# The level product of a fused convolution and attention kernel: fp32 products against three passes of rounded parts

## The reference

```python
x_aux = silu(conv1x1(gn(x), w_sta))                    # 128 channels
y1 = [x_aux]; y2 = [x_aux]
for _ in range(3):
    y1.append(0.9 * maxpool5(y1[-1]) + 0.1 * sumpool5(y1[-1]) / 25)
    y2.append(exp_weighted_pool5(y2[-1]))              # sum(e*x) / (sum(e) + 1e-6)
y = concat(silu(conv1x1(concat(y1), w_cv1)), silu(conv1x1(concat(y2), w_cv2)))
a = conv1x1(ddwv(ddwh(dwv(dwh(y)))), w_c1)             # four depthwise 3-tap convolutions first
x = x + silu(conv1x1(y * a, w_cvend))
f = tokens(gn(x))                                      # 1024 tokens of 256 channels
x = x + softmax((f @ w1.T) @ f.T / 16) @ (f @ w2.T)
```

## Time and profile before

| | us |
|---|---|
| median of 3 runs | 1432.04 |
| lowest, highest | 1429.85, 1433.74 |
| the profiled execution, its time | 1429.68 |
| the profiled execution, its span | 1427.9 |
| TensorE busy | 1273.4 (89%) |
| VectorE busy | 1148.8 (80%) |
| ScalarE busy | 704.6 (49%) |
| GpSimd busy | 159.5 (11%) |

### The profile page before, as it was taken

How to read it: one execution, slowest core, us unless ns; L and a number is a source line. 1 busy time by engine, 2 the same in 40 slices (tenths; PEclk the granted TensorE clock), 3 DMA queues, 4 the chain that set the end, 5 groups by cost and what they waited for, 6 DMA issues and landing times.

```text
span 1427.9 us, 18374 instructions
## 1 busy us (share of the span) xinstructions
PE 1273.4 (89%) x7162; PEld 1063.4 (74%) x7162; DVE 1148.8 (80%) x1217; ACT 704.6 (49%) x762; POOL 159.5 (11%) x76
## 2 busy tenths in 40 slices
PE   3569899836999998999899989999999999999697
PEld 1249899524878877987798679868986898688597
DVE  7879888595899879877987799779987988786443
ACT  0256768550365347435653566346534653564243
POOL 1657677100000000000000000000000000000000
PEclk9879999867999999999999999999999999999899
DMA  7311212110000100020002000200020002000000
GB/s 291 147 45 75 89 75 106 42 59 0 30 15 1 75 29 15 0 73 29 15 0 103 0 15 15 88 15 0 15 88 15 0 15 88 0 1 36 25 1 30
DMA packets 19176, 62.84 MB, mean 44 GB/s; under 512 B 1601, under 2 KB 4289, under 8 KB 19137
## 3 DMA queue, kind: packets, MB, share of 16 engines
q1 hardware_dynamic: 18432, 62.00, 11.5%
q10 hardware_dynamic: 704, 0.30, 0.1%
HBM read 36.61 MB, written 25.17 MB: 43 GB/s over the span
## 4 chain that ended last, share of the span: by engine, by line
PE 59%; issue 14%; DVE 14%; ACT 6%; DMA 0%; DVEq 0%; ACTq 0%; POOLq 0%; POOL 0%
PE slot L1126 21%; PE slot L1164 12%; PE ps_o L1164 9%; DVE between L1439 5%; PE slot L549 3%; PE slot L1180 3%; DVE a L1439 2%; PE slot L1104 2%; PE ps_e L549 2%; PE ps_ey L565 2%; PE slot L1151 1%; PE ps_ey L549 1%; DVE ps_e L766 1%; DVE x_all L773 1%; PE ps_t L642 1%
## 5 line engine op out<-in xcount | busy, mean ns | idle before, releaser
L1164 PE MATMUL slot<-f_all,q_all 128*128 128x512 f32 x768 | 195.4, 406 | 13.4 <-ACT pooled L1305 13.4
L1164 PE MATMUL ps_o<-v_all,pt_all 128*128 128x256 f32 x1536 | 199.1, 286 | 5.4 <-ACT mixed L1324 5.2
L1164 PEld LDWEIGHTS ps_o<-v_all,pt_all 128*128 128x128 f32 x1536 | 188.7, 191 | 7.7 <-DVE pt_all L1443 6.2
L1164 PEld LDWEIGHTS slot<-f_all,q_all 128*128 128x128 f32 x768 | 144.1, 193 | 43.6 <-ACT pooled L1305 14.8
L1439 DVE SCALAR_TENSOR_TENSOR a<-between,k_columns,a 128x992 f32<-128x992 f32 (+1 forms) x128 | 157.4, 1231 | 4.9 <-ACT a L1296 2.6
L1056 POOL TENSOR_TENSOR c_rstd<-c_spread,k_minus_half 128x2 f32<-128x2 f32 x8 | 5.6, 697 | 1087.0 <-DVE gmean L1509 1087.0
L1319 ACT CAST v_all<-y 128x1024 fp32r<-128x1024 f32 x32 | 33.7, 1052 | 184.6 <-DVE y L1470 184.6
L1443 DVE TENSOR_TENSOR pt_all<-slot,pt_all 128x1024 fp32r<-128x1024 f32 x64 | 78.1, 1221 | 46.9 <-ACT pt_all L1310 46.9
L1104 PE MATMUL slot<-wide,k_cv 128*128 128x512 f32 x256 | 114.3, 597 | 0.0
L1324 ACT ACTIVATE mixed<-ps_o,row_inv 128x256 f32<-128x256 f32 x64 | 30.3, 473 | 150.1 <-PE ps_o L1164 150.1
L1296 ACT ACTIVATE a<-between,k_columns 128x1024 f32<-128x1024 f32 x64 | 79.4, 1241 | 48.6 <-DVE between L1439 47.7
(11 more groups left out here) (166 smaller groups left out, 2725.0 us busy)
## 6 DMA issues: line engine op xcount, KB each, us to landing
levels<-x_all SPq DMA_DIRECT2D x32, 512.0 KB, 2.6
x_all<-in_x SPq DMA_DIRECT2D x8, 1024.0 KB, 13.3
q_all<-levels SPq DMA_DIRECT2D x8, 1024.0 KB, 4.9
x<-in_x SPq DMA_DIRECT2D x8, 1024.0 KB, 4.9
out<-x SPq DMA_DIRECT2D x8, 1024.0 KB, 3.9
pooled<-levels SPq DMA_DIRECT2D x8, 512.0 KB, 3.3
wide<-levels SPq DMA_DIRECT2D x7, 512.0 KB, 3.2
x_all<-in_w_c SPq DMA_DIRECT2D x2, 512.0 KB, 3.6
```

Source lines behind the costliest of these rows:

```text
L1164: last = nc.tensor.matmul(out, lhs, rhs, start=(n == 0), stop=(n == len(parts) - 1))
```

## The change

The `cv1` weights are split like the others into `cv1_hi` and `cv1_lo`: their load goes into a free half of image 5 behind the store of image 3, the scalings run on that copy after the last SiLU, then the cast, and GpSimd makes the low part last. Their fp32 copy is gone. In the third stage `cv1` becomes a `product_split` of 24 passes per tile, with `means()` behind the seventh of its twelve pairs. Level 0 is the pooled part 0, which is split already. Levels 1 to 3 are split at the end of the step before, three casts on ScalarE and three subtractions on VectorE, into v_all and pt_all (free once `cvend` is through); for image 0 this happens ahead of the steps. For level 0 to last through `cv1`, the buffers of two pairs are swapped: the pooled parts 0 and 2 now lie in q_all, 1 and 3 in f_all. The first low part of the taps in a step waits for the end of `cv1`. The scratch for dynamic DMAs is halved.

```diff
--- before.py
+++ after.py
@@ -48,8 +48,8 @@
 COLUMNS = {"b_sta": 1, "b_cv1": CT, "b_cv2": CT, "b_cvend": CT, "b_c1": KT,
            "taps": STAGES * KT * 3, "b_taps": STAGES * KT}
 
-SPLIT = {"w1": (CT, C), "w2": (CT, C), "cvend": (KT, C), "c1": (KT, C4), "cv2": (KT, C)}
-STAGED = {"w1": (0, 1, 0, 512), "w2": (0, 1, 512, 1024), "cvend": (1, 2, 0, 1024), "c1": (2, 4, 0, 1024), "cv2": (4, 5, 0, 1024)}
+SPLIT = {"w1": (CT, C), "w2": (CT, C), "cvend": (KT, C), "c1": (KT, C4), "cv2": (KT, C), "cv1": (KT, C)}
+STAGED = {"w1": (0, 1, 0, 512), "w2": (0, 1, 512, 1024), "cvend": (1, 2, 0, 1024), "c1": (2, 4, 0, 1024), "cv2": (4, 5, 0, 1024), "cv1": (5, 6, 0, 1024)}
 EXP_LN, SILU = "natural_log_exp_and_others", "silu_and_others"
 
 
@@ -116,6 +116,8 @@
         self.hi_done = counted("hi", LEVELS)
         self.lo_done = counted("lo", LEVELS)
         self.boxed = counted("boxed", LEVELS)
+        self.level_hi_done = counted("level_hi", LEVELS)
+        self.level_lo_done = counted("level_lo", LEVELS)
         self.borders = ctx.enter_context(nc.semaphore("chain_borders"))
         self.gate = ctx.enter_context(nc.semaphore("chain_gate"))
         self.n_borders = 2 + 2
@@ -231,6 +233,18 @@
                                                     image2d(self.work_b[:, :]), ALU.mult, ALU.add))
         own.wait()
 
+    def split_into(self, hi, lo):
+        self.hi, self.lo = hi, lo
+
+    def level_split_hi(self, act, i, level):
+        wait(act, self.done, i, MIX * level)
+        self.nc.scalar.copy(self.hi[:, level], self.wide[:, level]).then_inc(self.level_hi_done.sem, 1)
+
+    def level_split_lo(self, dve, i, level):
+        wait(dve, self.level_hi_done, i, level)
+        self.nc.vector.tensor_tensor(self.lo[:, level], self.wide[:, level], self.hi[:, level].bitcast(F32),
+                                     ALU.subtract).then_inc(self.level_lo_done.sem, 1)
+
     def mixture_of_sums(self, dve, level):
         wait(dve, self.summed, 0, 6 * (level + 1))
         self.mixture(dve, 0, level, self.sum_b[:, :, :])
@@ -250,7 +264,7 @@
     def __init__(self, ctx, nc, levels, chain):
         self.nc, self.chain = nc, chain
         self.second = ctx.enter_context(nc.sbuf_tensor("pooled", [P, N], F32))
-        self.shared = ctx.enter_context(nc.sbuf_tensor("q_all", [P, KT, N], F32R))
+        self.shared = ctx.enter_context(nc.sbuf_tensor("f_all", [P, KT, N], F32R))
         self.other = None
         self.second_in = Signal(ctx.enter_context(nc.semaphore("pooled_second_in")), 16)
         self.others_in = Signal(ctx.enter_context(nc.semaphore("pooled_others_in")), 16)
@@ -321,7 +335,7 @@
         ps_var = ctx.enter_context(nc.psum_tensor("ps_var", [P, HALF], F32))
 
         x_in = [sem(f"a_x_in{i}") for i in range(B)]
-        sta_in, cv1_in, box_in = sem("a_sta_in"), sem("a_cv1_in"), sem("a_box_in")
+        sta_in, box_in = sem("a_sta_in"), sem("a_box_in")
         weights_in = {k: sem(f"a_{k}_in") for k in SPLIT}
         stats_done = sem("a_stats_done")
         mv_done = sem("a_mv_done")
@@ -355,19 +369,24 @@
             for i in range(B):
                 sp.dma_start(x_all[:, i], x_v[i]).then_inc(x_in[i], 16)
             sp.dma_start(box_raw[:, :], consts["box"]).then_inc(box_in, 16)
-            sp.dma_start(keep["cv1"][:, :, :], rows("cv1")).then_inc(cv1_in, 16)
-            for k in SPLIT:
+            def load_weights(k):
                 sp.wait_ge(xn_done, STAGED[k][1] * CT)
                 n = STAGED[k][1] - STAGED[k][0]
                 for j in range(n):
                     sp.dma_start(raw[k][:, j].rearrange("p (t o) -> p t o", o=SPLIT[k][1]),
                                  w[k].rearrange("(n t p) o -> n p t o", p=P, n=n)[j]).then_inc(weights_in[k], 16)
 
+            for k in SPLIT:
+                if k != "cv1":
+                    load_weights(k)
+
             for n in range(B):
                 sp.wait_ge(stem_done, n + 3)
                 if n == 0:
                     sp.dma_start(chain.wide[:, 0], x_all[:, 0, 0]).then_inc(chain.loaded.sem, 16)
                 sp.dma_start(levels[n], x_all[:, n, 0]).then_inc(stored[n], 16)
+                if n == 3:
+                    load_weights("cv1")
 
         @block.scalar
         def _(act):
@@ -392,9 +411,6 @@
             act.wait_ge(chain.borders, chain.n_borders)
             chain.zero_first(act)
             silu(3)
-            act.wait_ge(cv1_in, 16)
-            for k in range(1, KT):
-                nc.scalar.mul(keep["cv1"][:, k], keep["cv1"][:, k], T_POOL ** k).then_inc(scaled_done, 1)
             split("w1")
             split("w2")
             silu(4)
@@ -404,6 +420,12 @@
             silu(6)
             split("cv2")
             silu(7)
+            act.wait_ge(weights_in["cv1"], 16)
+            for k in range(1, KT):
+                part = raw["cv1"][:, 0, k * C:(k + 1) * C]
+                nc.scalar.mul(part, part, T_POOL ** k).then_inc(scaled_done, 1)
+            act.wait_ge(scaled_done, KT - 1)
+            split("cv1")
             act.wait_ge(box_in, 16)
             nc.scalar.copy(box[:, :], box_raw[:, :]).then_inc(box_ready, 1)
             chain.zero_next(act, 1)
@@ -460,7 +482,7 @@
             inverse_deviations(1)
             chain.box_sums(pool, 0, 0)
             low_parts(("w1", "w2"))
-            low_parts(("cvend", "c1", "cv2"))
+            low_parts(("cvend", "c1", "cv2", "cv1"))
 
         @block.vector
         def _(dve):
@@ -821,7 +843,7 @@
 
 def kept_tensors(ctx, nc):
 
-    shapes = {"ident": [P, P], "group": [P, P], "cv1": [P, KT, C],
+    shapes = {"ident": [P, P], "group": [P, P],
               "columns": [P, sum(COLUMNS.values())], "minus_half": [P, B * CT]}
     keep = {k: ctx.enter_context(nc.sbuf_tensor("k_" + k, v, F32)) for k, v in shapes.items()}
     at = 0
@@ -885,9 +907,9 @@
 
 
 
-        f_all = sb("f_all", [P, KT, N], F32R)
-        q_all = pooled.shared
-        pooled.other = f_all
+        f_all = pooled.shared
+        q_all = sb("q_all", [P, KT, N], F32R)
+        pooled.other = q_all
         v_all = sb("v_all", [P, KT, N], F32R)
         pt_all = sb("pt_all", [P, KT, N], F32R)
         f_hi, f_lo = f_all[:, 0:CT], f_all[:, CT:KT]
@@ -895,6 +917,7 @@
         v_hi, v_lo = (v_all[:, k:k + CT].rearrange("p t (m c) -> p (t m) c", c=C) for k in (0, CT))
         pt_hi, pt_lo = pt_all[:, 0:2], pt_all[:, 2:4]
         a_hi, a_lo, y_hi, y_lo = f_all, q_all, v_all, pt_all
+        chain.split_into(v_all, pt_all)
         prob = pooled.second
         mixed = sb("mixed", [P, 2, C])
         between = sb("between", [P, 2, N])
@@ -1093,27 +1116,14 @@
                     box_sum(nc, pe, box, slot, zt_hi, zt_lo,
                             (chain.lo_done.sem, chain.lo_done.at(i, level + 1))).then_inc(chain.boxed.sem, 1)
 
-                def cv1(m, between=None):
-
-                    slot = claim("cv", CT + m)
-                    for h in range(2):
-                        for k in range(KT):
-                            if m == 0 and h == 0 and k:
-                                wait(pe, chain.done, i, MIX * k)
-                            rows = chain.wide[:, k, h * HALF:(h + 1) * HALF]
-                            last = nc.tensor.matmul(slot[:, h * HALF:(h + 1) * HALF], keep["cv1"][:, k, cols(m)], rows,
-                                                    start=(k == 0), stop=(k == KT - 1))
-                        if h == 0 and between:
-                            between()
-                    last.then_inc(cv.sem, 1)
-
                 def cols(m):
                     return slice(m * P, (m + 1) * P)
 
-                def product_split(kind, m, name, hi, lo, sig, order, hi_ready, lo_ready):
+                def product_split(kind, m, name, hi, lo, sig, order, hi_ready, lo_ready, between=None):
 
 
                     slot = claim(kind, m)
+                    m = m % CT if kind == "cv" else m
                     w_hi, w_lo = keep[name + "_hi"][:, :, cols(m)], keep[name + "_lo"][:, :, cols(m)]
                     parts = ((w_hi, hi, hi_ready), (w_lo, hi, hi_ready), (w_hi, lo, lo_ready))
                     uses = [(n, part) for part in parts for n in range(KT - 1)] + [(KT - 1, part) for part in parts]
@@ -1125,6 +1135,8 @@
                             hs = slice(h * HALF, (h + 1) * HALF)
                             last = nc.tensor.matmul(slot[:, hs], weights[:, k], inputs(k)[:, hs],
                                                     start=(at == 0), stop=(at == len(uses) - 1))
+                        if between and at == len(uses) // 2:
+                            between()
                     last.then_inc(sig.sem, 1)
 
                 def tiles_of(t):
@@ -1136,6 +1148,19 @@
                 def cv2(m):
                     product_split("cv", m, "cv2", pooled.hi, pooled.lo, cv, pooled.ORDER, when(pooled.hi_done),
                                   when(pooled.lo_done))
+
+                def cv1(m, between=None):
+                    def hi(k):
```

(25 more changed lines are left out.)

## The result

| | before | after |
|---|---|---|
| median, 7 runs each, us | 1432.04 | 1439.75 |
| lowest to highest | 1429.85 to 1434.12 | 1437.71 to 1444.01 |
| span of the profiled execution | 1427.9 | 1435.9 |
| TensorE busy in it | 1273.4 | 1263.3 |

The changed kernel is slower: ratio 1.0054, 95% interval 1.0036 to 1.0071. The forecast was 1432.0 us with a range of 1426.5 to 1437.0; the measured time lies above it. TensorE's busy time fell by 10.1 us only.

What follows compares the result with a forecast made beforehand. At image boundaries the path was taken to leave TensorE at the means for VectorE and ScalarE. Terms -1.7 + 1.1 + 1.8 = +1.2 us gave 1430.9, or 1433.2 from the median; forecast 1432.0, range 1426.5 to 1437.

Steps and rivals of the forecast that it cites:

- What bounds the kernel: At image boundaries only the level product's first 3.4 us, up to the means, are on the path; then VectorE and ScalarE.
- rival A: The saved TensorE time comes off in full, 22 us, 1409 us: 4%; a part of it, 1423 to 1427: 10%.
- The hook's gain of 0.24 us per boundary: Group means come after 14 passes, 3.20 us, instead of 4 fp32 products, 3.44 us: -1.7 us over seven boundaries.
- The added splits hidden: Three casts and three subtractions per image fit ScalarE's and VectorE's idle time before the means: cost nothing, cover 1.2 us.
- rival B: The subtractions' cover fails and VectorE reaches the means late: 1444 us halfway, 1457 wholly; 5%.
- The stem, +1.1 us: At the stem's end, GpSimd's added subtraction takes turns with VectorE's mixture over SBUF and delays the closing barrier 1.1 us.
- What was late next: After the means, VectorE's first outer tap; the level product's second tile ends 2.5 us earlier, which become a TensorE wait.
- The clock, +1.8 us: New idle time ahead of the query product lowers TensorE's clock in half of seven images, 0.5 us each; between 0 and 6.3.
- The old falls, expected 0: Existing clock falls at the score, in four of six images, may come or go: -6.4 to +3.2 us, expected 0.
- Rival C: Clock falls at the new idle place in all seven images, 0.9 us each, old falls become six: 1438.6 to 1441; 11%.
- Rival D: The new passes cost more than cv2's; the path sees it only if all 48 take over 0.29 us; under 1%.
- From the profiled execution to the median: The sum gives 1430.9 us from the profiled execution, 2.4 us under the median, or 1433.2 from the median; middle taken, 1432.0.

Runs made afterwards that it cites:

- The kernel with less work: The kernel before with 3 of the 16 fp32 products of each image's second level tile left out, nothing added: 1437.37 us, ratio 1.0015 to the kernel before.
- the second comparison: The changed kernel run once more, unaltered, against the kernel before: 1440.46 us against 1434.06, ratio 1.0049.

## Why the prediction was wrong, point by point

Between the two profiled executions the sum had +1.2 us and the measured difference is +8.0. The new falls gave 2.6 us more than their term, the old falls 3.2 and the last steps 1.8, where nothing was put down; the stem gave 1.2 less and the hook, with the seventh period, 0.4 less gain.

- **What bounds the kernel, and rival A.** Right. The level product's work beside the chain was worth nothing: 21 us less of it alone gave no gain.
- **The hook's gain of 0.24 us per boundary.** Right: 0.25 in the profile (139.32 against 139.57), 0.23 with no clock fall in either kernel.
- **The added splits hidden, rival B.** Right; the cover left was 1.52 us, forecast 1.2.
- **The stem, +1.1 us.** Right for the mixture: 1.02, and gone when the two engines don't meet. As a term of the sum it isn't borne out: the first means of the third stage came no later (-0.1 us), and that stretch differs by 7 us between traces.
- **What was late next.** Right in place, and near in size: the level product, with the group sums in it, takes 2.3 us less (forecast 2.5 to 2.8), TensorE waits 1.78 us for the rounded image (forecast 1.7 to 2.2) and then for the low part, 1.25 us as shown (the passes before that wait were slowed) and 1.43 at full clock (forecast 1.7).
- **The clock, +1.8 us.** This step failed: the price of a fall in this term, together with the old falls taken at 0 in the next. "A fall there costs at most 1.6 us of TensorE time" took the length of a fall from the score, where TensorE is busy once it has begun again. Here a second gap follows while the clock is low, and it stays low for 6.8 us, not 3.4. I priced a fall at 0.1 to 0.9 us on the path and took 0.5; with the second gap filled it measured 0.3, as a single fall, and with both gaps 1.3 to 1.7. Three such falls made +4.4 us, where the sum had +1.8 for three and a half. Their number was right by luck: no row bore on it.
- **The old falls, expected 0.** Also wrong, +3.2 us in the profile: the changed kernel showed the fall at the score in six of six images in both of its traces, the kernel before in four. The kernel with less work, which has both waits at the query product open as well, also showed six; the three variants of the changed kernel with one or both of them filled, and the one with the fp32 product, showed four or five. Whether the two places hang together isn't shown. Why the clock falls in all six here, and why in only two or three images at the query product, stays open; one execution of each variant was traced, two of the changed kernel.
- **Rival C**, at 11%, was the nearest: new falls, and the old ones in all six images. That its time (1438.6 to 1441) holds the measured 1439.75 is partly luck, for it had seven new falls of 0.9 us where there were three of 1.3 to 1.7, and the 1.8 us of the last steps was in no term. I had weighed two gaps of 1.7 us with work between as less than one of 2.23 us. In price they are near it, 1.3 to 1.7 us for each fall against 1.6; in number they are not, three images of seven against six of six.
- **Rival D** had a wrong bound. The path sees a dearer pass as soon as the 14 up to the means take more than the old 3.44 us, so from 0.246 us each, not from 0.29. It came to nothing: they took 3.18 us (669.17 to 672.35), 0.227 each.
- **From the profiled execution to the median.** I took the middle of 1430.9 and 1433.2. This was off by little: in the profiled executions the change cost 8.0 us, in the medians 7.7 and, in the second comparison, 6.4. The falls come and go between executions, so one trace is one draw: its low time in the kernel before was near 120 us, where the runs had 130 in the mean.

## What to carry to other kernels

Work taken from an engine that isn't on the path there buys nothing, and on TensorE it can cost: look where the freed time turns into idle time, whether dense work on the path follows it, and whether a second wait stands behind the first. If one does, price a clock fall with both waits. A few dummy products in such a gap (they gained 0.4% at the score alone, 0.9% in all here) are a cheap test for what the clock costs. Keep them to few instructions: 26 more in the loop's body cost nothing here, 44 more cost 2 us in each repetition.

## What the hardware showed that I had not expected

- A clock fall at the query product lasted 6.8 us where a second gap followed it, and 3.4 us with that gap filled.
- Two idle stretches at the query product, 1.78 and 1.13 to 1.44 us with the rounded image's four passes between them, came with a clock fall in three images of seven, in both traces of the changed kernel. The second alone (1.40 to 1.43 us) came with none in seven images. One of 2.23 us at the score came with a fall in four to six images of six.
- A loop body of TensorE with 22 more passes than the changed kernel's made it wait 2 us at the top of every repetition, with 73 instruction packets moved against 27; with 13 more passes it did not wait, with 28 packets.
- GpSimd's subtraction and VectorE's operation with two inputs in SBUF took turns, whole instruction by whole instruction: 2.23 us against 1.21 for the mixture.
